# Gating the token tiles in seven groups instead of nine, in a metaformer block with a routed FFN

## The chip, the cores and the metric

The kernel runs on one core of a Trainium2 chip. The metric is the device time of one execution in microseconds (us), median of several runs. Engines are named as in the profile: PE is TensorE (PEld its weight loads), DVE is VectorE, ACT is ScalarE, POOL is GpSimd and SP is SyncE.

## The reference, cut to what matters

x has the shape (T=4, B=32, N=49, C=128): 6272 tokens of 128 channels, 49 tiles of 128 tokens.

```python
x = x + conv_ref(_ln_c(x), ...)      # spiking attention: q, k, v, then y, then the output projection, each through lif over the images
t = x.reshape(B_, H_ * W_, C_)
t = t + ffn_ref(_ln_t(t), Wg, W1, b1, W2, b2)

# ffn_ref, over all tokens xt; E = 8 experts, K = 2, H = 512
gate = softmax(xt @ Wg)
topv, topi = top_k(gate, K)
topv = topv / (sum(topv) + 1e-06)
for e in range(E):
    h = gelu(xt @ W1[e] + b1[e])
    out = out + (h @ W2[e] + b2[e]) * scores[:, e:e + 1]
```

`lif` carries a state from each image of the sequence to the next, so the spikes come out in the order of the images. Only the two chosen experts of a token have a score that isn't zero.

## The kernel before, in words

The first half of the kernel walks over the images. 128 images of 49 tokens are cut into 16 blocks of 8 images (392 tokens). A loop over slots does in slot s the projections and the scan of block s for q, k and v, and, three slots later (LAG), the output projection and the last scan of block s - 3. VectorE carries the scan (the loop over `st` from L877): per image a sum (L879, or L881 once only the last column is left, from slot 16 on), a threshold (L889) and, in slots below 16, a product (L897). Each waits for the one before it. After every one of these 24 points of a slot the program puts in one small piece of other work, `norm_stage` and `gate_stage`, which is how norm and gate are hidden in the waits of the scan. In the slot's fifth step the y state of a block is worked on too (`spike_y`, L674 to L686), once its transpose by DMA (L345, issued by SyncE) has landed. A slot ends with the output spikes `osp` of a block (L912).

The second half is the routed FFN. Every token's normed row is scattered twice to `by_expert`, into the region of each of its two experts, 128 rows by one scatter (L427, GpSimd). Then a loop over 56 pieces of 256 rows loads a piece (L367, SyncE), turns it (L1154), multiplies it by W1 (L1167 to L1169) and W2 (L1177) of its expert and scatters the rows back to `by_token` (L443). SyncE starts these loads only after it has waited for all scatters of all groups (L360 to L362). The end sums the two shares of each token.

What connects the halves is done by groups of token tiles, and GATE_CUTS (L54) says which tiles form a group. For each group g:

- `norm2_block(g)` (L100) is the block in which its last tile ends, and `norm2_slot[g]` = that + 4 (L106) the first slot in which its output spikes are all there;
- in that slot: TensorE turns the spikes back (`turn_out`, L1092, the first work of TensorE in a slot), VectorE adds the residual (`add_residual`, L713), takes statistics of each tile (L647) and of the group (L627 to L640), ScalarE the root (L463), VectorE the reciprocal and the shift (L697, L701), ScalarE normalises tile by tile (`normalise`, L477), TensorE turns the rows, four tiles to an item (L1038), and ScalarE copies them to `xT` (L488). Each of these waits for the whole group or item ahead of it;
- one slot later (`gate_group(slot, 1)`): TensorE's `logits` (L1110), VectorE's `choose` (L735 to L773, from point 11 of the slot on) and TensorE's `count_before` (L1117, L1119), which stands behind the turns of the next group in TensorE's order (L1142 to L1145);
- two slots later: VectorE's `rank_rows` (L785 to L803), whose L797 and L801 write the places, and GpSimd's `scatter` (L419), two scatters for each tile.

Before, the norm slots of the nine groups are 6, 8, 11, 13, 15, 16, 17, 18 and 19, and the last ranks stand in slot 21. From slot 19 on there is no scan any more and the 24 points follow one another at once. GpSimd has nothing else to do in this stretch than these scatters. The rows to scatter lie in one of five buffers (`XG`, `place`; SENDING), and a group from the sixth on waits for the scatters of the group five before it.

Of the kernel before, what the change touches and what calls it, by code (L numbers as in the profile page):

```python
# [31 lines left out]
def metaformer_block(nc, x, Wq, Wk, Wv, Wp, bp, lif_w, Wg, W1, b1, W2, b2, out):  # L32
# [10 lines left out]
    TILES = TOK // 128  # L43
# [7 lines left out]
    SLOTS = BLOCKS + LAG  # L51
    assert C == 128 and TB == 128 and HID % 128 == 0 and TOK % (128 * R) == 0 and N <= NPAD and BC <= 512
    W = R * 128
    GATE_CUTS = [0, 7, 15, 23, 30, 36, 39, 42, 45, TILES]  # L54
    GR = max(b - a for a, b in zip(GATE_CUTS, GATE_CUTS[1:]))
    BT = BLOCKS // T
    CHOOSE_FROM = 11
# [21 lines left out]

    GATED = list(zip(GATE_CUTS[:-1], GATE_CUTS[1:]))  # L80
    GATES = len(GATED)
# [1141 lines left out]
```

## Time and profile before

| what | us |
|---|---|
| median of 3 runs | 534.23 (533.28 to 534.72) |
| span of the profiled execution, first to last instruction | 531.9 |
| PE busy | 346.8 |
| DVE busy | 384.5 |
| ACT busy | 305.1 |
| POOL busy | 222.5 |

The profile is of one execution, and gives its span, not its time with what lies around it; the median of the runs is 2.3 us above the span. The first half takes until about 292 us, the loop over pieces until about 510, the sum the rest. In a timeline row, the bracket at the end is the idle time of the engine just before it, and what ended it.

### The profile page before, as it was taken

The numbers are of one execution on the slowest core, as the hardware profiler recorded it, in microseconds if no ns is written. First come the engines' busy times: TensorE is split into PE (matmuls) and PEld (weight loads), VectorE is DVE, ScalarE is ACT, GpSimd is POOL, SyncE is SP. The second block draws the span as 40 slices with busy tenths as digits, with TensorE's granted clock in tenths as the row PEclk, the third lists the DMA queues.
The fourth block names the chain that finished last, engine by engine and source line by source line (L and its number), as shares of the span: only waits on it lengthen the run. The fifth ranks groups of instructions, "written<-read, shape, count | busy, mean of one in ns | idle before, by whom it ended". The sixth has DMA issues, their size and how long they took to land.

```text
span 531.9 us, 10740 instructions
## 1 busy us (share of the span) xinstructions
PE 346.8 (65%) x2516; PEld 287.3 (54%) x2516; DVE 384.5 (72%) x1368; ACT 305.1 (57%) x709; POOL 222.5 (42%) x233
## 2 busy tenths in 40 slices
PE   2466565657742758354410699999999999999200
PEld 1233233435421435242310599999999999999200
DVE  4699999998898798979770466666666666666186
ACT  3458684766647556362310477766666676776073
POOL 3000000027173037375777055666656566665400
PEclk9977777775576775655555699999999999999755
DMA  6901001102121011221542222222222222221299
GB/s 176 287 8 25 16 15 22 17 18 67 25 67 47 9 36 59 48 67 43 194 136 81 61 76 76 75 63 78 68 75 66 69 75 70 75 62 50 74 352 311
DMA packets 62123, 43.05 MB, mean 81 GB/s; under 512 B 29057, under 2 KB 56745, under 8 KB 62096
## 3 DMA queue, kind: packets, MB, share of 16 engines
q1 hardware_dynamic: 53648, 28.85, 20.5%
q0 software_dynamic: 6720, 12.97, 7.7%
q10 hardware_dynamic: 1728, 0.94, 0.7%
q8 instruction: 9, 0.15, 0.1%
q14 instruction: 18, 0.15, 0.1%
HBM read 22.09 MB, written 19.91 MB: 79 GB/s over the span
## 4 chain that ended last, share of the span: by engine, by line
PE 48%; DVE 35%; issue 5%; ACT 4%; POOL 3%; DMA 3%; ACTq 1%; POOLq 0%; SPq 0%; DVEq 0%
PE PS L1177 19%; DVE U L897 6%; PE PS L1167 6%; DVE VV L889 5%; DVE H_all L879 5%; PE PS L1169 5%; PE PS L1168 5%; PE PS L1110 3%; PE PS L1047 3%; POOL by_expert L427 3%; DVE stats L647 2%; PE PS L1154 2%; DVE X L1011 2%; PE PS L1038 2%; DVE spikes L907 1%
## 5 line engine op out<-in xcount | busy, mean ns | idle before, releaser
L427 POOL DMA_INDIRECT by_expert<-XG,place x98 | 97.9, 999 | 188.2 <-DVE place L801 159.9
L443 POOL DMA_INDIRECT by_token<-osp,target x112 | 119.8, 1069 | 88.5 <-DVE osp L981 55.5
L1177 PE MATMUL PS<-w_now,hid 128*128 128x128 f32 x896 | 108.8, 275 | 0.0
L1177 PEld LDWEIGHTS PS<-w_now,hid 128*128 128x128 f32 x896 | 104.8, 192 | 0.0
L577 ACT ACTIVATE hid<-PS,b1c 128x256 f32<-128x256 f32 x224 | 87.9, 480 | 5.3 <-PE PS L1169 3.1
L1167 PE MATMUL PS<-rows_high,w_high 128*128 128x256 f32 x224 | 68.5, 306 | 1.0 <-DVE rows_low L965 0.3
L583 ACT ACTIVATE w_now<-W_s 128x512 f32 x56 | 35.6, 635 | 53.6 <-PE PS L1177 44.7
L1169 PE MATMUL PS<-rows_high,w_low 128*128 128x256 f32 x224 | 63.7, 284 | 0.0
L1168 PE MATMUL PS<-rows_low,w_high 128*128 128x256 f32 x224 | 63.6, 284 | 0.0
L1047 PE MATMUL PS<-xT,wT 128*128 128x392 f32 x96 | 57.1, 722 | 0.7 <-ACT xT L488 0.7
L959 DVE CAST w_high<-H_all 128x512 fp32r x56 | 24.1, 430 | 39.4 <-PE PS L1169 38.1
L889 DVE SCALAR_TENSOR_TENSOR VV<-H_all 128x196 f32<-128x196 f32 (+2 forms) x152 | 50.2, 330 | 2.6
L879 DVE TENSOR_TENSOR H_all<-U,H_all 128x196 f32<-128x196 f32 (+1 forms) x128 | 44.9, 351 | 9.0 <-ACT H_all L500 6.1
L981 DVE TENSOR_TENSOR osp<-PS,b2b 128x256 f32<-128x256 f32 x56 | 23.8, 425 | 35.5 <-PE PS L1177 34.3
L897 DVE TENSOR_TENSOR U<-VV,OM 128x196 f32<-128x196 f32 (+1 forms) x128 | 44.8, 350 | 3.3 <-DVE VV L889 0.5
L1167 PEld LDWEIGHTS PS<-rows_high,w_high 128*128 128x128 f32 x224 | 42.9, 192 | 3.9 <-issue 3.3
L1168 PEld LDWEIGHTS PS<-rows_low,w_high 128*128 128x128 f32 x224 | 43.2, 193 | 0.0
L1169 PEld LDWEIGHTS PS<-rows_high,w_low 128*128 128x128 f32 x224 | 43.1, 192 | 0.0
L506 ACT ACTIVATE KVT<-PS 128x1024 bf16<-128x1024 bf16 x16 | 16.4, 1023 | 40.0 <-PE PS L1069 40.0
L963 DVE TENSOR_TENSOR w_low<-H_all,w_high 128x512 fp32r<-128x512 f32 x56 | 38.1, 680 | 0.0
L1154 PE MATMUL PS<-identf,rows_in 128*128 128x128 f32 x112 | 22.0, 279 | 24.4 <-DMA rows_in<-by_expert 24.4
L500 ACT ACTIVATE H_all<-PS,sg 128x392 f32<-128x392 f32 x48 | 27.8, 608 | 16.5 <-PE PS L1047 16.1
(156 smaller groups left out, 590.4 us busy)
## 6 DMA issues: line engine op xcount, KB each, us to landing
rows_in<-by_expert SPq DMA_DIRECT2D x56, 130.0 KB, 2.1
X<-in_x SPq DMA_DIRECT2D x7, 448.0 KB, 6.1
out<-X SPq DMA_DIRECT2D x7, 448.0 KB, 5.7
xT<-by_token SPq DMA_DIRECT2D x3, 896.0 KB, 7.3
H_all<-in_L_ffn_W SPq DMA_DIRECT2D x1, 2048.0 KB, 9.7
by_token<-osp,target POOLq DMA_INDIRECT x112
H_all<-by_token SPq DMA_DIRECT2D x2, 896.0 KB, 11.4
W_s<-by_token SPq DMA_DIRECT2D x2, 896.0 KB, 11.7
```

Source lines behind the costliest of these rows:

```text
L427: pool.indirect_dma_start(by_expert, bass.IndirectOffsetOnAxis(ap=place[g % SENDING][:, k, r:r + 1], axis=0), XG[g % SENDING][:, r, :], No ...
L443: pool.indirect_dma_start(by_token, bass.IndirectOffsetOnAxis(ap=target[b][:, a:a + 1], axis=0), rows_out[b][:, a, :], None, bounds_check= ...
L577: nc.scalar.activation(hid[b][:, hb, :], PS[:, hb, 0:ROWS], ACT.Gelu, bias=b1c[:, bass.ds(e * HB + hb, 1)]).then_inc(gelu_done, 1)
L879: m = do(v.tensor_tensor(h[:, cur, st, :], U[:, cur, :], h[:, cur, st, :], ALU.add))
L889: m = do(v.scalar_tensor_tensor(VV[:, cur, :], h[:, cur, st, :], 1.0, h[:, cur, st, :], ALU.is_lt, ALU.mult))
L897: m = do(v.tensor_tensor(U[:, cur, :], VV[:, cur, :], OM[:, cur, :], ALU.mult))
L963: v.tensor_tensor(w1_low[b % 2][:], w1, w1_high[b % 2][:].bitcast(F32), ALU.subtract).then_inc(w1_set, 1)
L1047: pe.matmul(bank[:, 0:BC], wT[:, w, :], xT[:, BC * b:BC * b + BC], start=True, stop=True).then_inc(ring_done, 1)
L1167: pe.matmul(PS[:, hb, 0:ROWS], high, rows, start=True, stop=False)
L1168: pe.matmul(PS[:, hb, 0:ROWS], high, rows_l, start=False, stop=False)
L1169: pe.matmul(PS[:, hb, 0:ROWS], low, rows, start=False, stop=True).then_inc(up_done, 1)
L1177: m = pe.matmul(PS[:, 4 + b % 2, a * 128:a * 128 + 128], hid[b % 2][:, hb, a * 128:a * 128 + 128], w2_now[b % 2][:, hb * C:hb * C + C], st ...
```

## The change

```diff
-    GATE_CUTS = [0, 7, 15, 23, 30, 36, 39, 42, 45, TILES]
+    GATE_CUTS = [0, 8, 15, 22, 29, 36, 43, TILES]
```

TILES is 49. The nine groups had 7, 8, 8, 7, 6, 3, 3, 3 and 4 tiles; the seven have 8, 7, 7, 7, 7, 7 and 6. The norm slots become 6, 8, 11, 13, 15, 18 and 19; the last ranks are in slot 21 as before. GR, the size of the largest group, stays 8, and with it all buffers. The number of scatters stays 98. Nothing else is changed.

## Rows read from the trace of the kernel before

**Rows 1.** Page, busy tenths in 40 equal slices of the span.
```profile
POOL 3000000027173037375777055666656566665400
PEclk9977777775576775655555699999999999999755
```

**Rows 2.** Chain of waits, and timeline of PE, at the loop's start: start, us, what.
```profile
290.75 2.27 DMA by_expert<-XG,place
...
296.28 0.69 PE L1154 MATMUL PS<-identf,rows_in 128*128 128x128 f32 x2 [23.86 <-DMA rows_in<-by_expert]
```

**Rows 3.** Timeline of POOL: start us, us, engine line op out<-in, count.
```profile
243.54 0.96 POOL L427 DMA_INDIRECT by_expert<-XG,place  x1 [4.54 <-DVE place L801]
...
290.75 0.95 POOL L427 DMA_INDIRECT by_expert<-XG,place  x1 [0.30 <-issue]
```

**Rows 4.** Timeline of DVE, slots 19 to 21.
```profile
262.18 0.18 DVE L735 TENSOR_REDUCE gate<-PS 128x3 f32<-128x24 f32 x1 [1.05 <-PE PS L1110]
...
266.21 0.18 DVE L785 TENSOR_TENSOR gate<-PS,filled 128x24 f32<-128x24 f32 x1 [1.39 <-PE PS L1119]
...
266.81 0.17 DVE L801 TENSOR_REDUCE place<-gate 128x3 int32<-128x24 f32 x1
```

**Rows 5.** Timeline of DVE, slots 16 and 17.
```profile
235.81 0.21 DVE L735 TENSOR_REDUCE gate<-PS 128x6 f32<-128x48 f32 x1 [2.24 <-PE PS L1110]
...
240.81 0.27 DVE L881 SCALAR_TENSOR_TENSOR H_all<-VV,osg,H_all 128x49 f32<-128x49 f32 x1 [0.17 <-ACT xT L488]
...
243.08 0.19 DVE L801 TENSOR_REDUCE place<-gate 128x6 int32<-128x48 f32 x1
...
245.31 0.62 DVE L674 SCALAR_TENSOR_TENSOR HY<-VY,osg,y_turned 128x392 f32<-128x392 f32 x1
...
249.22 0.53 DVE L912 TENSOR_SCALAR osp<-H_all 128x392 bf16<-128x392 f32 x1
```

**Rows 6.** Timeline of DVE, slot 18.
```profile
250.34 0.56 DVE L713 TENSOR_TENSOR X<-PS,X 128x384 f32<-128x384 bf16 x1
...
252.87 0.27 DVE L881 SCALAR_TENSOR_TENSOR H_all<-VV,osg,H_all 128x49 f32<-128x49 f32 x1
...
253.17 0.21 DVE L889 SCALAR_TENSOR_TENSOR VV<-H_all 128x49 f32<-128x49 f32 x1
...
253.42 0.16 DVE L640 SCALAR_TENSOR_TENSOR ln<-ln 128x3 f32<-128x3 f32 x1
...
254.74 0.16 DVE L701 SCALAR_TENSOR_TENSOR ln<-ln 128x3 f32<-128x3 f32 x1
```

**Rows 7.** Timeline of SP, and the landing of that transpose's line.
```profile
240.58 1.12 SPq L345 DMA_TRANSPOSE y_turned<-y_rows  x1
...
DMA to landing us min/median/max: 2.3/2.4/2.7
```

**Rows 8.** Chain of waits, a group of seven tiles in slot 13.
```profile
188.24 0.94 PE PS L1098 x7
189.21 1.10 DVE X L713
```

**Rows 9.** Timeline of DVE, slot 19, a group of four tiles.
```profile
258.55 0.69 DVE L713 TENSOR_TENSOR X<-PS,X 128x512 f32<-128x512 bf16 x1 [0.29 <-PE PS L1098]
...
259.38 0.28 DVE L647 BATCH_NORM_STATS2 stats<-X 128x6 f32<-128x128 f32 x1
...
260.96 0.16 DVE L640 SCALAR_TENSOR_TENSOR ln<-ln 128x4 f32<-128x4 f32 x1
```

**Rows 10.** Timeline of ACT, four tiles normalised.
```profile
262.90 1.65 ACT L477 ACTIVATE XG<-X,ln 128x128 f32<-128x128 f32 x4 [1.45 <-DVE ln L701]
```

**Rows 11.** Timeline of PE, a group of seven tiles, slots 13 to 15.
```profile
200.68 1.73 PE L1038 MATMUL PS<-identf,XG 128*128 128x128 f32 x7 [2.54 <-ACT XG L477]
...
205.60 3.15 PE L1110 MATMUL PS<-Wg_s,xT 128*128 128x8 f32 x14
...
214.67 0.32 PE L1119 MATMUL PS<-chosen,all_ones 128*128 128x56 bf16 x7
```

## The prediction, made before the changed kernel ran

> **What bounds the kernel now.** I began with the slices of the page. Each is 13.3 us. GpSimd (POOL) is busy by fits at first, at 7 tenths in a row from slice 19 to 21 (counted from 0), and at 0 in slice 22; TensorE is granted 0.5 of its clock there, its 1.2 GHz level, and 0.9 from slice 23 on [rows 1]. So a stretch ahead of the piece loop seems to wait for GpSimd. The chain of waits says for what: its last item before the loop is the landing of a scatter issued at 290.75 us, and the first matmul of the loop runs at 296.28, after 23.86 us of idle TensorE [rows 2]. SyncE may load no piece before every scatter has landed (the waits on `scattered`), so what ends the first half is the last scatter's end at 290.75 + 0.95 = 291.70.
>
> The timeline of GpSimd shows how it came there [rows 3]. At 243.54 it starts on group 4, after an idle of 4.54 us that ended with that group's places. From there 38 scatters run back to back: 12 of group 4, then 6, 6, 6 and 8 of groups 5 to 8. Their starts lie (290.75 - 243.54) / 37 = 1.276 us apart. The short groups are what keeps this queue fed: when one is sent, the places of the next are there already (group 7's at 266.97 [rows 4], when GpSimd still had 19 scatters to start).
>
> **What the change does, by slots.** A group takes its norm in slot `norm2_slot`, its choice in the next slot, its ranks and scatters in the one after. Before, the norm slots are 6, 8, 11, 13, 15, 16, 17, 18, 19; after, 6, 8, 11, 13, 15, 18, 19. Up to tile 36 there are five groups in the same slots either way, of 8, 7, 7, 7, 7 tiles in place of 7, 8, 8, 7, 6. Every product, statistic and scatter of a tile stays, so I cost this part at nothing: the tiles sum to 36 both times, and GpSimd idles between these groups. Places in `by_expert` count tiles in order, so the piece loop gets the same rows. Tiles 36 to 38, 39 to 41 and 42, which were normed in slots 16, 17 and 18, now form group 5 in slot 18; its norm can't start before slot 17 has written its spikes. GpSimd then has 14 + 14 + 12 = 40 scatters left from group 4 on, and it will run dry between groups 4 and 5 unless group 5's places come in time. The sum is the time of those places.
>
> Slot 16. VectorE's choice for group 4 waits until 235.81 for its logits [rows 5]. The logits get one tile more, 0.45 us by the 3.15 that seven take (slot 19 below), but `turn_out` of a three-tile group, about as long, no longer runs ahead of them: no difference. Behind the wait three norm operations go: slot 17 starts 0.35 us earlier, at 240.45 for 240.81 [rows 5].
>
> Group 4's places came at 243.27 [rows 5], in the midst of group 6's residual. Without that they come some 0.7 earlier; GpSimd's 14 scatters are out by 243.54 + 14 x 1.276 = 261.4 at the latest.
>
> Slot 17 keeps eight scan steps of two operations and the y state; the norm and choice of short groups go. Scan operations follow one another at 0.30 us (252.87 to 253.17 [rows 6]) with a small one between; I take 0.31. That is 16 x 0.31 = 5.0, plus 1.0 for the y state (0.62 [rows 5] and the spikes behind it) and 0.4 for the output spikes. They end at 246.9, where they ended at 249.22 + 0.53 = 249.75: 2.85 us gained. Its cover is thin: the y block's transpose is issued at 240.58 and lands 2.3 to 2.7 later [rows 7], at 242.9 to 243.3, and the scan asks for it at about 243.1.
>
> Slot 18, group 5 with seven tiles. Turning its spikes takes 0.94 and its residual 1.10 [rows 8]: 249.05. In the old slot 18 the last operation on the norm's statistics (L640) started at 253.42, 2.5 after the residual's end at 250.90, with three tiles [rows 6]. Four more tiles add 4 x 0.2 (a statistic takes 0.28 [rows 9], part of it in waits of the scan), while ranks and choice of the short groups leave this slot and give about 0.3 back: 252.05. From there to the shift's end (254.74 + 0.16) was 1.48 [rows 6]; without the choice between I take 1.25: ScalarE starts at 253.3. It normalises at 1.65 / 4 = 0.41 a tile [rows 10]: 256.2. TensorE turns seven tiles in 1.73 [rows 11], to 258.05. Both steps get their seven tiles whole, since each waits for the whole group.
>
> Slot 19. TensorE runs in order: `turn_out` of group 6 (0.85, a little under the 0.94 of seven tiles) and then group 5's logits, 3.15 [rows 11]: 262.15. ScalarE's copy of the second turn to `xT` is done beside `turn_out`; if that cover goes, the logits start about one ScalarE operation, 0.4, later. VectorE's residual and statistics took from 258.55 to 260.96 with four tiles [rows 9]; two more make it 2.41 + 0.26 + 2 x 0.28 = 3.2, from 259.0 to 262.3. The choice runs from there: twelve operations of 0.21 [rows 5], each behind the last, 2.7 us with their gaps, to 265.0. It isn't the last wait: `count_before` of group 5 stands in TensorE's order behind group 6's turns. The shift of group 6 ends at 263.0, ScalarE takes 6 x 0.41, to 265.6, the turns 1.5, to 267.15, and the counts about 0.6 (the sums over seven tiles 0.32 [rows 11]), to 267.8.
>
> Slot 20. The ranks took 266.21 to 266.97 for three tiles [rows 4]; with seven 0.85: places at 268.75, and GpSimd starts 0.27 later as at group 4: **269.0**. It has idled some 8 us by then. Group 6's places follow at about 275, long before its turn comes at 286.9, so 26 scatters run through: 269.0 + 25 x 1.276 + 0.95 = 301.85. The last scatter ends **10.1 us later** than at 291.70. The tables for the pieces, the first weights and W1 were there some 10 us before the loop, and at worst move by 2 us: hidden. The loop itself starts at the lower clock level in both, after an idle of TensorE of over 20 us [rows 2], and is the same work: nothing.
>
> **A rule against the trace.** Three-tile operations of the choice take 0.18 us and six-tile ones 0.21 [rows 4, 5], so almost all of one, 0.15, is fixed, and 60 such operations go with two groups. In the steps above most of them were filling waits of the scan.
> The Trainium skill, Perfetto Trace Analysis, "Optimizing Scalar/DVE Operations", gives about 60 ns of such overhead for VectorE on SBUF and says that grouping helps if the engine is saturated. By its figure 60 x 0.06 = 3.6 us would be an estimate of the gain, 540.7 if all came off the path. The same section says that where VectorE is not saturated but makes others wait, breaking instructions up may let work finish sooner; that speaks against this change, and the idle of VectorE before 262.18 and 266.21 [rows 4] agrees.
>
> **Rivals.**
> (a) Group 5 is late by another 3 to 5 us, places at 271.5 to 273.5: the y block holds slot 17, its scan stays as long as before (2.85 back), or the round between engines is slower for seven tiles than I add. For it: the thin cover above. Against: nothing that was priced by hand is large. 547 to 549.
> (b) GpSimd never runs dry: places by 261.4, then the queue only has two scatters more, 40 for 38, and 2 x 1.276 = 2.6 us: 536.8. It would need group 5 to be 7.4 us quicker than my steps. The single waits of slots 18 and 19 on ScalarE and TensorE don't give that.
> (c) Faster. VectorE is the engine that sets the pace until slot 18, and taking 60 operations of 0.15 us, 9 us, off it lets everything in slots 16 to 19 come that much sooner, in the places that matter. It decides only where group 5's places come by 257 (12 us before my 268.75) and group 4's 14 scatters begin by 239: then the last scatter ends at 257.3 + 32.85 = 290.1, and the time is 532.6. Against it: the choice of group 4 waits for logits until 235.81 whatever VectorE does.
> (d) The edit does nothing that counts: if the last scatter were not what SyncE waits for, the time would stay at 534. The chain excludes it almost.
>
> **The numbers.** The profile lists a span of 531.9 us; the median of the runs is 534.23, 2.3 more, for what lies around it. I add the difference to both: 531.9 + 10.1 = 542.0 for the span, 534.2 + 10.1 = 544.3 us. Chances: forecast 0.70 (places 264.5 to 271.5, 540 to 547), (a) 0.20, (b) 0.05 with what lies between it and the forecast, (c) 0.02, (d) 0.03. The range, 539.5 to 549, takes in forecast and (a) but for the far end. A measurement of this kernel can tell some 0.3%, 1.6 us, from no change: faster 0.02 (c), same 0.03 (d), slower 0.95.
>
> **What would show it.** GpSimd's timeline after: 14 scatters from about 243, an idle of 6 to 10 us that ends with places (L801), then 26 without a break that end near 301.9. VectorE's output spikes of slot 17 end near 247, not 249.75; ScalarE's seven normalisations start near 253; group 5's logits end near 262. The pause of TensorE before its first L1154 grows from 24 us to about 29. It is wrong if GpSimd shows no idle after group 4 (b), or if the first part up to 235 has moved by more than 1 us, which I cost at nothing, or if the loop's length changes.

## The result, and the profile after

The changed kernel takes 543.27 us (median of 4 runs, 539.58 to 546.73), the kernel before 534.48 in the runs beside them: a ratio of 1.0177, with a 95% interval from 1.0135 to 1.0218, or 7 to 12 us more. The forecast was 544.3. Medians here and below are over all executions of a kernel, while ratios, intervals and the ranges named with them leave out the few that fell in a slower state (front alone once, 548.78 us; seven groups fed earlier once, 666.25; the even ten groups once, 532.49; the kernel before once, 662.87).

The profiled execution after is the quickest of the four, 539.58 us with a span of 537.8. GpSimd's timeline after, around the gap between group 4 and group 5, and at its end (start us, us, engine, line, operation, then the idle time before it and what ended it):

```profile
237.61 0.96 POOL L427 DMA_INDIRECT by_expert<-XG,place  x1 [4.29 <-DVE place L801]
...
254.06 0.95 POOL L427 DMA_INDIRECT by_expert<-XG,place  x1 [0.31 <-issue]
264.20 0.96 POOL L427 DMA_INDIRECT by_expert<-XG,place  x1 [9.18 <-DVE place L801]
...
296.27 0.95 POOL L427 DMA_INDIRECT by_expert<-XG,place  x1 [0.30 <-issue]
```

Where [rows 3] had 38 scatters without a break, there are now 14 (from 237.61), an idle of 9.18 us that group 5's places end, and 26 that end at 296.27 + 0.95 = 297.22. The loop over pieces is moved as a whole. Its turns, before and after (the row gives first and last start):

```profile
L1154 PE MATMUL PS<-identf,rows_in x112: 272/273/477, 296.3 to 487.0; 128*128 128x128 f32 x112
```

```profile
L1154 PE MATMUL PS<-identf,rows_in x112: 270/273/475, 301.9 to 492.6; 128*128 128x128 f32 x112
```

From its first to its last turn it takes 190.7 us both times. From the last scatter's end to the end of the span it is 240.2 before and 240.6 after, so nothing of the difference lies behind the scatters.

One thing must be read with care. The last scatter ends 297.22 - 291.70 = 5.5 us later in these two profiles, and not the 9 that the medians differ by, because everything up to slot 16 ran 4.8 us earlier in the second. VectorE's output spikes of slots 15 and 16, before:

```profile
229.62 0.37 DVE L912 TENSOR_SCALAR osp<-H_all 128x392 bf16<-128x392 f32 x1
240.29 0.36 DVE L912 TENSOR_SCALAR osp<-H_all 128x392 bf16<-128x392 f32 x1
```

and after:

```profile
224.16 0.37 DVE L912 TENSOR_SCALAR osp<-H_all 128x392 bf16<-128x392 f32 x1
235.49 0.35 DVE L912 TENSOR_SCALAR osp<-H_all 128x392 bf16<-128x392 f32 x1
```

The same first half takes another time in other executions (section on hardware below), so this shift is mostly not the edit's. I therefore measure the tail from the start of slot 16's output spikes to the end of the last scatter. Before that is 291.70 - 240.29 = 51.4 us, after 297.22 - 235.49 = 61.7. The 10.3 between them is what the change does behind slot 16. What it does ahead of that point is small, and is taken up with the prediction.

### The profile page after: what moved, and what is told of

Read it like the earlier page. It is cut to its first block, busy times and chain, and to the rows that moved or that the text cites. A ratio compares the mean times of both kernels' runs of the same rounds, so it can differ in the third digit from the quotient of the medians.

```text
span 537.8 us, 10656 instructions
## 1 busy us (share of the span) xinstructions
PE 337.3 (63%) x2514; PEld 282.9 (53%) x2514; DVE 380.7 (71%) x1308; ACT 304.4 (57%) x707; POOL 222.8 (41%) x233
## 4 chain that ended last, share of the span: by engine, by line
PE 45%; DVE 36%; ACT 5%; issue 5%; POOL 4%; DMA 3%; ACTq 1%; POOLq 0%; SPq 0%; DVEq 0%
PE PS L1177 19%; DVE U L897 6%; DVE VV L889 6%; PE PS L1167 6%; DVE H_all L879 6%; PE PS L1169 5%; PE PS L1168 5%; POOL by_expert L427 4%; DVE stats L647 3%; ACT XG L477 2%; PE PS L1154 2%; PE PS L1038 2%; PE PS L1047 2%; DVE X L1011 2%; PE PS L1110 2%
## 5 line engine op out<-in xcount | busy, mean ns | idle before, releaser
L1047 PE MATMUL PS<-xT,wT 128*128 128x392 f32 x96 | 52.7, 672 | 0.7 <-ACT xT L488 0.7
L1154 PE MATMUL PS<-identf,rows_in 128*128 128x128 f32 x112 | 22.0, 279 | 32.0 <-DMA rows_in<-by_expert 32.0
L961 DVE CAST rows_high<-PS 128x256 fp32r<-128x256 f32 x56 | 23.3, 416 | 23.2 <-PE PS L1154 23.2
```

The source lines that it names most:

```text
L1047: pe.matmul(bank[:, 0:BC], wT[:, w, :], xT[:, BC * b:BC * b + BC], start=True, stop=True).then_inc(ring_done, 1)
```

## The experiments

The theory: the first half ends with GpSimd's last scatter; scatters cost 1.27 us each where the queue runs without a break, and one more costs nothing where it would idle; the change leaves it without work until group 5's places, and these are a chain through all engines. The rivals: the number or size of the groups costs by itself; the new front (8, 7, 7, 7, 7 tiles) has a part in the time; the end is set by something else than the queue.

**Front alone.**

```diff
-    GATE_CUTS = [0, 7, 15, 23, 30, 36, 39, 42, 45, TILES]
+    GATE_CUTS = [0, 8, 15, 22, 29, 36, 39, 42, 45, TILES]
```

> Cuts 0, 8, 15, 22, 29, 36, 39, 42, 45, 49: the first five groups as after, the four short ones at the end as before. Theory (GpSimd's last scatters decide, the front costs nothing): group 4 has 14 scatters in place of 12 and the queue still never runs dry, so 40 in a row for 38: about 2.6 us over the kernel before, 536 to 538. Rival (regrouping the front gives the 4.9 us by which slot 16 ended earlier in the profile after): 530 to 533, and slot 16's osp (L912) ends near 235.8 in every run.

Measured: 535.33 us against 534.36 (ratio 1.0028, interval 0.9991 to 1.0064; runs from 531.5 to 539.1). The tail is 297.14 - 243.21 = 53.9 us, the expected 2.5 over 51.4. The median is only 1 us up, below the 536 that I expected at least, and the interval, -0.5 to 3.4 us, holds the 2.6, but doesn't show it. What it excludes is a gain of 4.9: slot 16's spikes are written at 243.21 here, later than in either of the first two profiles, though the cuts up to tile 36 are those that had 235.49.

**Tail alone.**

```diff
-    GATE_CUTS = [0, 7, 15, 23, 30, 36, 39, 42, 45, TILES]
+    GATE_CUTS = [0, 7, 15, 23, 30, 36, 43, TILES]
```

> Cuts 0, 7, 15, 23, 30, 36, 43, 49: the front as before, the tail as after. Theory: GpSimd idles 8 to 10 us after group 4's 12 scatters (11 to 12, as there are two less), places of group 5 some 28 us after slot 17 starts, then 26 scatters: 8.5 to 10.5 us over the kernel before, 543 to 545. Rival (front's 4.9 us was part of the change): slower still than the changed kernel by 4 to 5 us, 547 to 549.

Measured: 543.39 us (ratio 1.0196, 1.0157 to 1.0236), the same as the whole change. The tail is 299.98 - 238.43 = 61.6 us. GpSimd's gap is longer by the two scatters that group 4 has less, and ends with the same event:

```profile
267.02 0.96 POOL L427 DMA_INDIRECT by_expert<-XG,place  x1 [11.22 <-DVE place L801]
```

So the loss is in the tail, and whether group 4 has 12 or 14 scatters doesn't matter once the queue waits behind it.

**Work put into the gap, and the same work behind it.** Four more scatters, which write the group's first two tiles to a tensor that nobody reads; in one kernel behind group 4, in the other behind group 5.

```diff
+    EXTRA = {4: 2}        # or {5: 2}
...
-                for r in range(GATED[g][1] - GATED[g][0]):
+                n = GATED[g][1] - GATED[g][0]
+                for to, r in [*((by_expert, r) for r in range(n)), *((aside, r) for r in range(EXTRA.get(g, 0)))]:
                     for k in range(2):
-                        pool.indirect_dma_start(by_expert, bass.IndirectOffsetOnAxis(
+                        pool.indirect_dma_start(to, bass.IndirectOffsetOnAxis(
```

> The changed kernel with four more scatters behind group 4's (its first two tiles again, to a tensor that nobody reads). Theory (GpSimd idles about 9 us between group 4 and group 5, so work there is free): the idle shrinks by 4 x 1.27 = 5.1 us to about 4, and from slot 16's output spikes to the last scatter's end it stays 61.7 us (within 0.7); time as the changed kernel, 541 to 546. Rival (GpSimd's amount of work decides): 66.8 us there, and 546 to 551.

> The same four scatters more, behind group 5's instead. Theory (from group 5's places on the queue runs without a break and ends the first half): from slot 16's output spikes to the last scatter's end 61.7 + 5.1 = 66.8 us, time 5 us over the changed kernel, 546 to 551. Rival (the end is set by the chain through group 6's places, or by VectorE's tables): 61.7 and no more time.

GpSimd's timeline with the four in the gap (lines are three further down in this file):

```profile
261.94 0.95 POOL L430 DMA_INDIRECT by_expert<-XG,place  x1 [0.30 <-issue]
263.20 0.96 POOL L430 DMA_INDIRECT aside<-XG,place  x1 [0.30 <-issue]
...
266.99 0.96 POOL L430 DMA_INDIRECT aside<-XG,place  x1 [0.30 <-issue]
271.60 0.96 POOL L430 DMA_INDIRECT by_expert<-XG,place  x1 [3.65 <-DVE place L804]
...
303.62 0.96 POOL L430 DMA_INDIRECT by_expert<-XG,place  x1 [0.30 <-issue]
```

In the gap: the idle shrinks to 3.65 us, the tail is 304.58 - 243.00 = 61.6 us, as without them, and the time 545.56 (539.42 to 546.77; ratio 1.0177, 1.0115 to 1.0240), the ratio of the change itself (the median is 2.3 us above the changed kernel's, inside the spread of both). Behind group 5: the tail is 306.54 - 239.92 = 66.6 us, and the time 550.75 (547.92 to 553.05; ratio 1.0319, 1.0264 to 1.0373). GpSimd's timeline there:

```profile
268.52 0.96 POOL L430 DMA_INDIRECT by_expert<-XG,place  x1 [8.70 <-DVE place L804]
...
305.58 0.96 POOL L430 DMA_INDIRECT by_expert<-XG,place  x1 [0.31 <-issue]
```

In the tail, the same four scatters cost nothing in one place and 5 us in the other, and the executions' times of the two kernels don't overlap. This shows that the queue ends the first half and that its gap is real slack.

**One wait taken off group 5's places.** TensorE counts group 5 ahead of group 6's turns.

```diff
+                if slot >= SLOTS:
+                    for g in gate_group(slot, 1):
+                        count_before(g)
                 for it in ring[slot][1]:
                     ring_item(it)
-                for g in gate_group(slot, 1):
-                    count_before(g)
+                if slot < SLOTS:
+                    for g in gate_group(slot, 1):
+                        count_before(g)
```

> The changed kernel, where from slot 19 on TensorE does count_before ahead of the turns of the next group. Theory (group 5's places wait 2 us behind group 6's turns, as the prediction says): the count starts as soon as the choice ends, about 260.3 in place of 262.29 of the profile after, places 2 us earlier, the last scatter too: 59.7 us from slot 16's output spikes in place of 61.7, time 1.5 to 2 less than the changed kernel. Rival (something else holds the places): 61.7.

TensorE's timeline of slot 19, first in the changed kernel, then in this one:

```profile
254.10 3.10 PE L1110 MATMUL PS<-Wg_s,xT 128*128 128x8 f32 x14
260.62 1.51 PE L1038 MATMUL PS<-identf,XG 128*128 128x128 f32 x6 [3.42 <-ACT XG L477]
262.29 0.21 PE L1117 MATMUL PS<-chosen,before 128*128 128x64 bf16 x1
```

```profile
261.71 3.10 PE L1110 MATMUL PS<-Wg_s,xT 128*128 128x8 f32 x14
267.89 0.23 PE L1117 MATMUL PS<-chosen,before 128*128 128x64 bf16 x1 [3.08 <-DVE chosen L769]
```

From the logits' start to the count it was 8.19 us and is 6.18; the gap of GpSimd falls to 6.71 and the tail to 302.72 - 243.22 = 59.5 us, 2.2 less. The median, 541.67 (ratio 1.0150, 1.0105 to 1.0196), is 1.6 under the changed kernel, but the intervals overlap: it is the trace that shows this step, not the time.

**Seven groups, fed earlier.**

```diff
-    GATE_CUTS = [0, 7, 15, 23, 30, 36, 39, 42, 45, TILES]
+    GATE_CUTS = [0, 7, 15, 23, 30, 36, 42, TILES]
```

> Cuts 0, 7, 15, 23, 30, 36, 42, 49: seven groups of six to eight tiles as after, but the sixth ends at tile 42, so it is normed in slot 17 and not 18. Theory (what counts is when GpSimd is fed, not how many groups there are): places of group 5 at about 259, as GpSimd ends group 4; 38 scatters nearly in a row: within 2 us of the kernel before, 533 to 537. Rival (groups of six and seven tiles are slow through the round of engines, or the number of groups counts): 541 or more.

Measured: 542.41 us (ratio 1.0140, 1.0092 to 1.0188). The time is the rival's; the trace splits it. The tail is 296.93 - 241.39 = 55.5 us, 4.1 over the kernel before and 6.2 under the change. The rest, 4.5, is in the loop over pieces, which takes 195.2 us from first to last turn (189.2 to 191.7 in the profiles of all the other kernels):

```profile
L1154 PE MATMUL PS<-identf,rows_in x112: 272/273/476, 301.6 to 496.8; 128*128 128x128 f32 x112
```

I had put group 5's places at 259, 18 us into a tail that starts at about 241, and the queue without a gap. They came 22.3 us into it. VectorE's timeline of slots 18 and 19 shows where:

```profile
251.72 0.27 DVE L881 SCALAR_TENSOR_TENSOR H_all<-VV,osg,H_all 128x49 f32<-128x49 f32 x1 [0.88 <-ACT H_all L497]
...
256.15 0.21 DVE L735 TENSOR_REDUCE gate<-PS 128x6 f32<-128x48 f32 x1 [1.99 <-PE PS L1110]
...
260.04 0.21 DVE L785 TENSOR_TENSOR gate<-PS,filled 128x48 f32<-128x48 f32 x1 [0.23 <-PE PS L1119]
260.83 1.09 DVE L713 TENSOR_TENSOR X<-PS,X 128x896 f32<-128x896 bf16 x1 [0.59 <-PE PS L1098]
261.96 0.21 DVE L789 TENSOR_TENSOR gate<-gate 128x48 f32<-128x48 f32 x1
```

Three waits that I had left out: the scan's input stands behind six normalisations on ScalarE (0.88), the choice waits for six tiles' logits (1.99), and the second operation of the ranks stands behind group 6's residual (1.7). GpSimd idled 2.75 us, and group 4's own places came 1.3 us later as well. So feeding earlier gives back 6 of the 10 us with the same number of groups: the number isn't the cause. The closest pair for this is the tail-alone kernel, whose cuts differ by tile 42 only: 61.6 and 55.5. It is the traces that show it; the times, 543.39 and 542.41, don't. And it doesn't give all, since a group of six waits longer at the engines than one of three, as these three rows show.

**What the loop's 4.5 us were.** The same cuts, with small memsets of an unused tile at VectorE's start:

```diff
+            for i in range(8):        # or 32
+                v.memset(idle_work[:, i:i + 1], 0.0)
             first_norm()
```

> The third run's kernel (cuts 0, 7, 15, 23, 30, 36, 42, 49) with eight small memsets of an unused tile at VectorE's start, under 1 us in all. In the profile of the third run the loop over pieces takes 195.2 us from its first to its last turn (L1154), 190.7 in the others, with one long VectorE operation (L959, 0.72 for 0.43) in each round of four pieces. Theory (that is an accident of where VectorE's loop lies in its program, and has nothing to do with the groups): a shift of eight instructions can take it away: 190.7. Rival (it comes with the cuts, by the order of rows or what is left on a queue): 195.2 again.

> The same with 32 memsets, in case eight shift it by too little. Theory of the place in the program: at least one of the two loops takes 190.7 us. Rival: both 195.2.

The first operation of VectorE's round of four pieces, and the loop's turns, with eight:

```profile
L962 DVE CAST w_high<-H_all x49: 426/427/495, 311.0 to 478.4; 128x512 fp32r x49
```

```profile
L1157 PE MATMUL PS<-identf,rows_in x112: 272/273/474, 301.3 to 490.9; 128*128 128x128 f32 x112
```

That operation's longest was 718 ns in the kernel without the memsets, where eleven of its 56 took 0.7 us or more:

```profile
L959 DVE CAST w_high<-H_all x47: 426/428/718, 311.2 to 476.9; 128x512 fp32r x47
```

The loop takes 189.6 us with eight memsets and 189.2 with 32, and the tails stay at 296.66 - 241.09 = 55.6 and 292.07 - 236.18 = 55.9. The times, of one execution each, were 537.92 and 532.65. So the same cuts have a quick loop as well, and the slow one doesn't come with them. Whether it belongs to that build or to the one execution that was profiled is not shown: four of its executions lie between 541.67 and 543.55 us, which speaks for the build, and a fifth took 537.78. That it would be the place of VectorE's loop in its program is argued only. By the tails, then, these cuts cost about 4 us, not 8.

**More groups.** Two versions that feed the queue earlier still.

```diff
-    GATE_CUTS = [0, 7, 15, 23, 30, 36, 39, 42, 45, TILES]
+    GATE_CUTS = [0, 7, 15, 23, 30, 33, 36, 39, 42, 45, TILES]
```

> Cuts 0, 7, 15, 23, 30, 33, 36, 39, 42, 45, 49: as before, with group 4 split in two halves, the first normed in slot 14. Theory (before, the end of the first half is a backlog of 38 scatters that starts with group 4's places): six scatters run in GpSimd's idle time before 243.5, 32 are left: 7 us less, 526 to 530. Rival (a further group costs VectorE and TensorE what it saves GpSimd): 533 to 537.

Measured: 530.82 us (ratio 0.9933, 0.9911 to 0.9955): faster, by 3.5 us and not by 7. The tail is 288.58 - 240.67 = 47.9 us, 3.5 under the kernel before. The queue runs without a break, but already from group 3 on:

```profile
222.28 0.96 POOL L427 DMA_INDIRECT by_expert<-XG,place  x1 [5.17 <-DVE place L801]
...
287.62 0.96 POOL L427 DMA_INDIRECT by_expert<-XG,place  x1 [0.30 <-issue]
```

In the kernel before, GpSimd idled 4.54 us ahead of group 4 [rows 3], with group 3's 14 scatters just in front. Six scatters, 7.6 us, can't be hidden in 4.54, so at most 4.5 us were to be had; I had counted a whole slot as idle. The second version takes the surplus from the groups ahead too:

```diff
-    GATE_CUTS = [0, 7, 15, 23, 30, 36, 39, 42, 45, TILES]
+    GATE_CUTS = [0, 8, 15, 21, 27, 33, 36, 39, 42, 45, TILES]
```

> Cuts 0, 8, 15, 21, 27, 33, 36, 39, 42, 45, 49: ten groups, the middle ones of six tiles in slots 10, 12 and 14. Theory (in the ten groups of the fourth run GpSimd ran without a break from group 3's places in slot 15 on, 52 scatters; here group 4's come in slot 16 and 44 are left, 9 us later and 8 x 1.27 = 10.2 less): about 1 us less than that run, 528 to 531. Rival (small groups in full slots cost VectorE more than they give): 532 to 536.

```profile
204.52 0.96 POOL L427 DMA_INDIRECT by_expert<-XG,place  x1 [11.33 <-DVE place L801]
...
229.77 0.96 POOL L427 DMA_INDIRECT by_expert<-XG,place  x1 [9.63 <-DVE place L801]
...
284.99 0.95 POOL L427 DMA_INDIRECT by_expert<-XG,place  x1 [0.30 <-issue]
```

Measured: 528.44 us (ratio 0.9878, 0.9820 to 0.9937), the fastest of all here, 6 us under the kernel before. Forty-four scatters run from 229.77 on, as expected. Its distance to the other ten-group version lies inside the intervals and stays open; part of it may be the early front of its runs.

## Why the prediction was right

The forecast was +10.1 us and a time of 544.3; measured were 543.27 and, by the tails, +10.3. Taking slot 17's first scan operation as the zero (predicted at 240.45, in the profile after at 236.02), its steps stand so:

| step | predicted, us after slot 17 starts | measured |
|---|---|---|
| output spikes of slot 17 end | 6.45 | 6.50 |
| ScalarE starts to normalise group 5 | 12.85 | 12.51 |
| seven turns end | 17.60 | 17.19 |
| group 5's logits end | 21.70 | 21.18 |
| count of group 5 ends | 27.35 | 26.68 |
| group 5's places | 28.30 | 27.91 |
| last scatter ends | 61.40 | 61.20 |

Each is within 0.7 us. VectorE's and ScalarE's rows of the profile after, for slots 17 to 19:

```profile
242.09 0.43 DVE L912 TENSOR_SCALAR osp<-H_all 128x392 bf16<-128x392 f32 x1
...
243.54 1.09 DVE L713 TENSOR_TENSOR X<-PS,X 128x896 f32<-128x896 bf16 x1 [0.35 <-PE PS L1098]
...
254.34 0.96 DVE L713 TENSOR_TENSOR X<-PS,X 128x768 f32<-128x768 bf16 x1 [3.67 <-PE PS L1098]
...
262.74 0.22 DVE L785 TENSOR_TENSOR gate<-PS,filled 128x56 f32<-128x56 f32 x1 [2.46 <-PE PS L1119]
```

```profile
248.53 2.80 ACT L477 ACTIVATE XG<-X,ln 128x128 f32<-128x128 f32 x7 [0.54 <-DVE ln L701]
```

They answer to [rows 4 to 6]. VectorE, which had no pause over 0.4 us in slot 18 before, now stands idle 3.67 us for TensorE and 2.46 for the count.

The front, the slots up to 16, was put at nothing, and that is right as a sum, and not slot by slot. The tail alone gives 543.39 and the whole change 543.27. But slot 16, forecast 0.35 us shorter, came out longer: from slot 15's output spikes to its own 235.49 - 224.16 = 11.33 us, for 240.29 - 229.62 = 10.67 before, and 11.35 or 11.36 in the three other profiles with these seven groups. TensorE was granted 0.50 of its clock in it both times. The step that was wrong is that seven tiles in group 4, with no three-tile turn ahead of them, make no difference to the logits. VectorE's choice had them 230.85 - 224.16 = 6.69 us after slot 15's spikes, for 235.81 - 229.62 = 6.19 before [rows 5]. The table and the tail start behind this and don't see it:

```profile
230.85 0.22 DVE L735 TENSOR_REDUCE gate<-PS 128x7 f32<-128x56 f32 x1 [4.01 <-PE PS L1110]
```

That it doesn't show in the time is partly that terms cancel. In the slots that take the norm of groups 0, 1, 2 and 4 (slots 6, 8, 11 and 15) the length from spikes to spikes follows the tiles: 0.43 us more for one tile more, 0.45 less and 0.45 less for one fewer, 0.25 more for one more. With slot 16's 0.66 that is 0.4 us in all; slots 7, 9, 12 and 14 differ between executions by more than such a term.

The other steps, the rivals and the signs:

- One of the signs of being wrong that I had named did show: the first part up to 235 had moved by more than 1 us, by 4.8 to the earlier side. It isn't a part of the change, as the front-alone run and the other profiles with these cuts show, but the forecast time agrees with the median of several executions and not with the profiled one; had only that one run, 539.58 us, been taken, it would have read 5.4 us. The sign was badly chosen: nothing before the result told how much the first part varies by itself.
- Slot 17 shorter by 2.85 us: it ended 6.50 us after its start, where the kernel before took 249.75 - 240.81 = 8.94. The y block did not hold it: L674 ran without a wait at 238.85, and group 5's places were not late, so rival (a) did not come about.
- The count behind the turns: shown by moving it, 2.2 us.
- Rival (b), a queue that never runs dry: refuted by the idle of 9.18 us. Rival (c), VectorE's saved operations ahead of everything: group 5's places came 27.9 us after slot 17's start, and would have had to come 257 - 240.45 = 16.6 after it. They could not, because VectorE waits for others on the way.
- Rival (d), that the scatters are not the end: refuted by the four scatters behind group 5, +5 us.
- TensorE's pause before its first L1154 was 31.44 us, for the 29 that I gave: its own work ended earlier beside the scatters than I had it. It costs nothing.
- The rule and the trace: VectorE's busy time fell from 384.5 to 380.7 us, so the 60 small operations did save nearly the 3.6 us estimated from the Trainium skill's figure (Perfetto Trace Analysis, "Optimizing Scalar/DVE Operations"). None of it came off the end. The 0.15 us for each that I read from the rows, 9 us in all, is not borne out: the rows' durations overlap (in slot 18 after, L627 lasts 0.19 from 246.50 and the next operation starts at 246.62), so that a row can be longer than what its operation adds. The Trainium skill's other sentence, that breaking instructions up may let work finish sooner where VectorE makes others wait, agrees with the traces: GpSimd waits for VectorE's places, and the ten-group versions, with more and smaller operations, are quicker.

What the prediction did not have is the spread: it gave one front to both kernels, and the four runs of the changed one lie over 7 us. Those of the kernel before lie over 6 where there are many of them (529.59 to 535.62 in 23). That the forecast is within 1.0 us of the median is therefore partly luck; the steps of the table are the better evidence.

## What to carry to other kernels

Where small groups at the end feed a serial queue, the question is not what a group costs but whether its work is there when the queue asks: price the chain from the last input to the queue's first item, and compare it with the work that is still queued. Larger groups save operations on an engine with slack and pay with the whole group's latency at every hand-over between engines. To test such a reading, put the same dummy work once into the supposed gap and once behind it.

## What the runs showed of the hardware

The front is not the same in every execution. Four profiles have the same cuts up to tile 36 and the same instructions until slot 16: the changed kernel, the two with extra scatters, and the one with the moved count. Slot 16's output spikes are written at 235.49, 243.00, 239.92 and 243.22 us in them, and TensorE's granted clock between 100 and 200 us was 0.76, 0.66, 0.70 and 0.64 of full speed. Most of the difference lies in three slots. From spikes to spikes, slots 7, 9 and 12 take 13.91, 13.35 and 15.82 us in the changed kernel and 16.93, 15.82 and 17.72 in the one with the moved count, 7.4 of the 7.7 us. Slot 7 in the two (length, busy time of PE, PEld, DVE, ACT and POOL, then the granted clock, DMA share and GB/s):

```profile
98.18:112.09 13.91, 9.51 (x61) 6.30 (x60) 13.10 (x60) 10.60 (x26) 0.00 (x0) 0.75 0.09 16
```

```profile
97.89:114.82 16.93, 13.15 (x61) 8.69 (x60) 13.20 (x60) 10.62 (x26) 0.00 (x0) 0.50 0.08 13
```

The work is the same, and VectorE's and ScalarE's busy times nearly so. TensorE's is 3.64 us longer at 0.50, its 1.2 GHz level, all through the slot. VectorE waits for it there, directly for the logits and through ScalarE's root, which stands at 108.61 behind a copy (L500, 108.12) that waited for TensorE's products:

```profile
105.31 0.23 DVE L735 TENSOR_REDUCE gate<-PS 128x8 f32<-128x64 f32 x1 [1.41 <-PE PS L1110]
108.93 0.20 DVE L697 RECIPROCAL ln<-ln 128x7 f32<-128x7 f32 x1 [2.19 <-ACT ln L463]
```

In the changed kernel's slot 7 the first wait isn't there and the second is 0.67. So a stage in which VectorE is the busiest engine still gets longer with TensorE's lower clock, in the few places where it waits for TensorE. Why the clock falls in one execution and not in the next stays open. The mean clock of a whole execution tells less: the changed kernel took 539.58 us at 0.792 and 546.73 at 0.769, but 541.53 at 0.770. The one pair of profiles alone would have given 5.5 us for this change and not 9 to 10.

The second is the loop that ran 4.5 us longer in one profile and not in those of the same cuts with eight or 32 memsets some 300 us ahead of it. What makes it slow was not found. A difference of this size in a loop whose code was not touched is no evidence about the edit.
